# One adaLN block on one core: the shared PSUM steps in a new order, both output projections at the end of the second block, blocks of 9, 10, 9 and 8 steps

## The reference, cut to what matters

```python
mod = (silu(c) @ wmod).reshape(32, 6, 1, 128)       # sa, ca, ga, sb, cb, gb for each batch
ga, gb = sign(.) * max(abs(.), 0.25)
h = layernorm(x) * (1 + ca) + sa
q, k, v = h @ Wq, h @ Wkv                           # 16 heads of 64
s = (q * 64**-0.5) @ k.T;  p = exp(s - rowmax(s)), 0 above the diagonal
x = x + ga * ((p @ v / (sum(p) + 1e-8)) @ Wo + bo)
h = layernorm(x) * (1 + cb) + sb
fp4(t): per 16 channels scale = max|t| / 6; round t / scale to {0, .5, 1, 1.5, 2, 3, 4, 6}; times scale
gate, up = fp4(h) @ fp4(w_gate).T, fp4(h) @ fp4(w_up).T       # 352 hidden channels
x = x + gb * (fp4(silu(gate) * up) @ fp4(w_down).T)
```

## Time and profile before

| what | value |
|---|---|
| median of 3 runs | 1419.69 us (1419.22 to 1420.4) |
| the profiled execution's own time | 1420.77 us |
| its span from first to last instruction | 1418.8 us |
| granted TensorE clock, mean | 0.982 of full speed |
| PE (matmul) busy | 1268.3 us, 89% |
| DVE (VectorE) busy | 1010.3 us, 71% |
| ACT (ScalarE) busy | 836.0 us, 59% |
| POOL (GpSimd) busy | 826.5 us, 58% |
| exponentials, L559 ACT | 1024, mean 432 ns |
| row maxima, L730 DVE | 256, mean 1219 ns |
| normalisation, L429 and L431 POOL | 256 of mean 400 ns and 768 of mean 462 ns |

### The profile page before, as it was taken

One profiled execution on the slowest core, in us unless ns is written; L12 is line 12 of the kernel. 1 busy time (PEld: TensorE's weight loads), 2 busy tenths in 40 slices (PEclk: granted clock), 3 DMA queues, 4 the chain that ended last, 5 costly groups with the idle time before them and its releaser, 6 DMA issues.

```text
span 1418.8 us, 34191 instructions
## 1 busy us (share of the span) xinstructions
PE 1268.3 (89%) x10194; PEld 1045.9 (74%) x10194; DVE 1010.3 (71%) x2565; ACT 836.0 (59%) x2885; POOL 826.5 (58%) x1582
## 2 busy tenths in 40 slices
PE   5989999999999999999999999999999999999963
PEld 3778777777877777877777877777787777787752
DVE  5667777777777777777777777777777777777664
ACT  3666655665655656656666665566566565665630
POOL 2545656655656666655566565665565656665543
PEclk9999999999999999999999999999999999999985
DMA  3000000000000000000000000000000000000000
GB/s 96 16 18 19 8 20 20 17 20 20 4 20 20 17 20 20 7 18 20 20 17 20 19 5 20 20 17 20 20 4 20 20 17 20 20 6 14 18 18 10
DMA packets 38057, 26.54 MB, mean 19 GB/s; under 512 B 2800, under 2 KB 33392, under 8 KB 38032
## 3 DMA queue, kind: packets, MB, share of 16 engines
q1 hardware_dynamic: 38032, 26.23, 6.5%
HBM read 21.94 MB, written 4.28 MB: 18 GB/s over the span
## 4 chain that ended last, share of the span: by engine, by line
POOL 48%; issue 36%; PE 8%; DVE 3%; ACT 2%; POOLq 2%; DMA 1%; SPq 0%; DVEq 0%; ACTq 0%
POOL probs L431 21%; POOL qy L75 6%; POOL qy L73 5%; POOL probs L429 5%; POOL hq L77 3%; PE ps_m L818 2%; POOL rstd L439 2%; POOL h2a L469 2%; POOL xq L77 1%; POOL x_keep L486 1%; POOL x_gb L459 1%; PE ps_s L913 1%; PE ps_o L940 1%; PE ps_m L797 1%; PE ps_m L864 1%
## 5 line engine op out<-in xcount | busy, mean ns | idle before, releaser
L559 ACT ACTIVATE probs<-ps_s,neg_max 128x128 f32<-128x128 f32 (+1 forms) x1024 | 426.0, 432 | 404.9 <-PE ps_s L922 404.9
L431 POOL TENSOR_SCALAR probs<-probs,r_den 128x256 f32<-128x256 f32 (+1 forms) x768 | 341.8, 462 | 0.0
L429 POOL TENSOR_TENSOR probs<-probs,r_den 128x128 f32<-128x128 f32 x256 | 102.5, 400 | 401.8 <-DVE r_den L739 401.8
L730 DVE TENSOR_REDUCE neg_max<-ps_s 128x4 f32<-128x1024 f32 x256 | 304.2, 1219 | 20.2 <-PE ps_s L913 17.2
L656 DVE COPY probs_t<-ps_m 128x512 f32<-128x512 f32 x256 | 176.3, 689 | 134.4 <-PE ps_m L797 134.4
L913 PE MATMUL ps_s<-qk 64*128 64x256 f32 x2048 | 258.3, 391 | 0.4 <-ACT qk L525 0.4
L797 PE MATMUL ps_m<-ident,probs 128*128 128x128 f32 x1536 | 232.4, 274 | 3.9 <-DVE probs_t L656 2.4
L913 PEld LDWEIGHTS ps_s<-qk 64*128 64x128 f32 x2048 | 188.3, 188 | 42.8 <-ACT probs L559 10.9
L559 ACT ACTIVATION_READ_ACCUMULATOR probs<-ps_s,neg_max 128x1 f32 x1024 | 219.2, 214 | 0.0
L940 PE MATMUL ps_o<-probs_t,v 128*64 128x256 f32 (+1 forms) x2048 | 196.0, 333 | 14.3 <-ACT o_t L551 14.3
L940 PEld LDWEIGHTS ps_o<-probs_t,v 128*64 128x64 f32 x2048 | 132.3, 137 | 91.5 <-issue 58.5
(11 more groups left out here) (107 smaller groups left out, 1695.0 us busy)
## 6 DMA issues: line engine op xcount, KB each, us to landing
mod_a<-mod_rows SPq DMA_DIRECT2D x32, 256.0 KB, 3.4
x_in<-L_attn_x SPq DMA_DIRECT2D x32, 128.0 KB, 2.1
x_res<-L_attn_x SPq DMA_DIRECT2D x32, 128.0 KB, 2.1
out<-y_out SPq DMA_DIRECT2D x32, 128.0 KB, 2.9
mod_b<-mod_rows SPq DMA_DIRECT2D x32, 64.0 KB, 3.0
wkv<-L_attn_Wkv SPq DMA_DIRECT2D x2, 512.0 KB, 7.1
wq<-L_attn_Wq SPq DMA_DIRECT2D x1, 512.0 KB, 4.0
wo<-L_attn_Wo SPq DMA_DIRECT2D x1, 512.0 KB, 8.4
```

The costliest lines, as they stand in the source:

```text
L429: nc.gpsimd.tensor_tensor(cols, cols, r_den[:, u % 4, 0:1].to_broadcast([P, P]), ALU.mult)
L431: ins = nc.gpsimd.tensor_scalar(cols, cols, r_den[:, u % 4, s:s + 1], 1.0, ALU.mult, ALU.mult)
L559: ins = nc.scalar.activation(probs[:, u % 4, h, t * P:(1 + 2 * t) * P], ps_s[:, 2 * (u % 2) + h, t * N:t * N + (1 + t) * P], ACT.Exp, bias ...
L730: nc.vector.tensor_reduce(neg_max[:, u % 4, :], ps_s[:, 2 * (u % 2):2 * (u % 2) + 2, :].rearrange("p b (t j) -> p (b t) j", t=2), AX.X, AL ...
```

## The change

The order of the shared steps, of the reads that follow them, and of the other work of ScalarE, VectorE and GpSimd is changed. The instructions, their sizes, the DMA list and the number of shared steps (36) are the same. Both wo steps stand at the end of block 1; blocks have 9, 10, 9 and 8 steps. In blocks 1 to 3 the third t comes before the second qk. On VectorE, the second layer norm's statistics and xn2 move ahead in block 2, both hidden_scales and hidden_magic follow later steps of their blocks, and the quantisation of h2 comes before the reads of down. On GpSimd the rounding of xq moves from block 0 of the next iteration to the end of block 3, rounding of the hidden halves from blocks 2 and 3 to blocks 1 and 3, and h2 from block 3 to block 2. On ScalarE the copy of o_t in block 1 comes later, in block 2 it comes before xt. The three steps that prepare the feed-forward weights (once, in iteration 1) take other places.

```diff
-        PLACES = {
-            (0, 3): ("xqt", 2, 0), (0, 4): ("v", 0, 0), (0, 7): ("gate", 2, 0), (0, 8): ("up", 2, 0),
-            (1, 3): ("wo", 1, 0), (1, 4): ("gate", 2, 1), (1, 7): ("v", 0, 1), (1, 8): ("up", 2, 1),
-            (2, 3): ("wo", 1, 1), (2, 4): ("v", 0, 2), (2, 7): ("v", 0, 3), (2, 8): ("xt", -1, 0),
-            (3, 3): ("hqt", 2, 0), (3, 4): ("hqt", 2, 1), (3, 7): ("down", 2, 0), (3, 8): ("down", 2, 1)}
...
+        SHARED = (
+            ("t0", "qk0", "t1", ("v", 0, 0), ("xqt", 2, 0), "qk1", "t2", ("gate", 2, 0), ("v", 0, 1)),
+            ("t0", "qk0", "t1", ("up", 2, 0), ("gate", 2, 1), "t2", "qk1", ("up", 2, 1), ("wo", 1, 0), ("wo", 1, 1)),
+            ("t0", "qk0", "t1", ("v", 0, 2), ("hqt", 2, 0), "t2", "qk1", ("v", 0, 3), ("xt", -1, 0)),
+            ("t0", "qk0", "t1", ("hqt", 2, 1), "t2", "qk1", ("down", 2, 0), ("down", 2, 1)))
...
+        WEIGHT_PLACES = [(0, 7), (1, 3), (1, 4)]
...
-                    if j == 0 and has.prev2:
...
-                        quantize_round(nc.gpsimd, Steps(pool, xq_round, ROUND_STEPS, i - 2), xq, 2 * P // BLOCK, scale[0],
-                                       qy[0], qm[0])
...
-                    if j in (2, 3) and has.prev2:
-                        round_hidden(i - 2, j - 2)
-                    if j == 3 and has.prev:
+                    if j == 2 and has.prev:
+                        rstd(i - 1, ln2_pool, x1_steps, X1_STEPS * i, mv2, var2, rstd2)
+                    if j in (1, 3) and has.prev2:
+                        round_hidden(i - 2, (j - 1) // 2)
...
+                    if has.attn:
+                        normalize(i, 2 * j)
...
+                    if j == 2 and has.prev:
                         pool.wait_ge(xn2_ready, 2 * i)
...
+                    if j == 3 and has.prev:
+                        pool.wait_ge(xq_steps, QUANT_STEPS * i)
+                        if has.prev2:
+                            pool.wait_ge(xqt_full, i - 1)
+                        quantize_round(nc.gpsimd, Steps(pool, xq_round, ROUND_STEPS, i - 1), xq, 2 * P // BLOCK, scale[0],
+                                       qy[0], qm[0])
...
                         exponentials(2 * j, 1)
-                    if has_out and j == 1:
-                        out_copy()
-                    for n in (0, 1, 2, 3):
+                    first = 5 if j == 2 else 4
+                    for n in range(first):
                         shared_reads(n)
                     if has.attn:
                         exponentials(2 * j + 1, 0)
-                    shared_reads(4)
-                    shared_reads(5)
+                    for n in range(first, 6):
+                        shared_reads(n)
+                    if j == 1 and has.prev:
+                        out_copy()
                     if has.attn:
                         exponentials(2 * j + 1, 1)
-                    for n in (6, 7, 8):
+                    for n in range(6, 8):
                         shared_reads(n)
-                    if has_out and j != 1:
+                    if j != 1 and has.unit(2 * (j - 2)):
                         out_copy()
+                    for n in range(8, len(SHARED[j])):
+                        shared_reads(n)
...
                     shared_reads(j, 0)
+                    if j == 2 and has.prev:
+                        dve.wait_ge(x1_steps, X1_STEPS * (i - 1) + 2)
+                        layer_norm_stats(x1, stats2, mv2, x1_steps, X1_STEPS * (i - 1) + 2)
                     shared_reads(j, 2)
+                    shared_reads(j, 3)
                     if has.attn:
                         denominators(2 * j)
...
+                    shared_reads(j, 4)
+                    if j == 1 and has.prev2:
+                        hidden_scales(i - 2, 0)
                     if j == 0 and has.next:
...
+                    if j == 1 and has.prev2:
+                        hidden_magic(i - 2, 0)
+                    if j == 2 and has.prev2:
+                        hidden_scales(i - 2, 1)
+                    if j == 2 and has.prev:
+                        dve.wait_ge(ln2_pool, 2 * i)
+                        normalized([xn2[:, t * P:t * P + P] for t in range(2)], x1, mv2, rstd2, xn2_ready)
+                    if j == 2 and has.prev2:
+                        hidden_magic(i - 2, 1)
                     if j == 1 and has.next:
...
                     if j == 3 and has.prev:
                         dve.wait_ge(h2_ready, i)
...
+                    for n in range(5, len(SHARED[j])):
+                        shared_reads(j, n)
```

More of the change, by code:

```diff
@@ L301, in iterations, with place_of @@
                 body(i)
-        PLACES = {
[3 rows of a table removed]
-            (3, 3): ("hqt", 2, 0), (3, 4): ("hqt", 2, 1), (3, 7): ("down", 2, 0), (3, 8): ("down", 2, 1)}
[L309 to L316, removed]
+        SHARED = (
[4 rows of a table added]
+        def place_of(j, step):
+            part = int(step[-1]) if isinstance(step, str) else 0
+            if not isinstance(step, str):
+                return step
+            if step[0] == "t":
+                return ("t", 0, 3 * (j - 1) + part) if j > 0 else ("t", 1, 3 * (PAIRS - 1) + part)
+            return ("qk", 0, 2 * (j + 1) + part) if j < PAIRS - 1 else ("qk", -1, part)
+        PLACES = {(j, n): place_of(j, step) for j in range(PAIRS) for n, step in enumerate(SHARED[j])}
+        assert len(PLACES) % 3 == 0
+        WEIGHT_PLACES = [(0, 7), (1, 3), (1, 4)]
         def shared_steps(i):
@@ L487, in body @@
                     if j == 2 and has.prev:
-                        rstd(i - 1, ln2_pool, x1_steps, X1_STEPS * i, mv2, var2, rstd2)
+                        pool.wait_ge(xn2_ready, 2 * i)
+                        xn2_v, h2a_v, h2_v = (t[:, :].rearrange("p (t c) -> p t c", t=2) for t in (xn2, h2a, h2))
+                        nc.gpsimd.tensor_tensor(h2a_v, xn2_v, both_tiles(mod_a[:, 2, :]), ALU.mult).then_inc(h2a_ready, 1)
+                        pool.wait_ge(h2a_ready, i)
+                        if has.prev2:
+                            pool.wait_ge(xq_steps, QUANT_STEPS * (i - 1))
+                        nc.gpsimd.tensor_tensor(h2_v, h2a_v, both_tiles(mod_a[:, 3, :]), ALU.add).then_inc(h2_ready, 1)
+                    if j == 3 and has.prev:
+                        pool.wait_ge(xq_steps, QUANT_STEPS * i)
+                        if has.prev2:
+                            pool.wait_ge(xqt_full, i - 1)
+                        quantize_round(nc.gpsimd, Steps(pool, xq_round, ROUND_STEPS, i - 1), xq, 2 * P // BLOCK, scale[0],
+                                       qy[0], qm[0])
             def round_hidden(b, k):
@@ L546, in out_copy @@
                     def out_copy():
-                        if j == 2 and has.prev:
-                            act.wait_ge(wo_full, 2 * i)
                         at = 2 * ((j - 2) % PAIRS)
@@ L563, in exponentials @@
                         ins.then_inc(exp_done, 1)
-                    has_out = has.unit(2 * (j - 2))
                     if has.attn:
@@ L767, in body @@
                         normalized([xn[:, t, :] for t in range(2)], x_in, mv1, rstd1, xn_ready)
[L768 to L776, removed]
                     if j == 3 and has.prev:
@@ L958, in body @@
                         mask(2 * j + 1, 1)
-                    for n in range(2, 9):
+                    for n in range(2, len(SHARED[j])):
                         at_place(j, n)
```

10 lines of the change are left out of this document (removed).

## The result

| | before | after |
|---|---|---|
| median | 1420.05 us | 1362.88 us |
| ratio, 95% interval | | 0.9599 (0.958 to 0.9618) |
| profiled span | 1418.8 us | 1359.9 us |
| granted clock, mean | 0.982 | 0.988 |

What follows compares the result with a forecast made beforehand. TensorE's idle time was taken as the bound. Period 38.0 + 0.2 + 0.15 + 1.6 = 40.0 us against 42.15, 2.1 less over 30 periods (63 us), plus 4 in the drain: 1354 us, range 1318 to 1387.

Steps and rivals of the forecast that it cites:

- What bounds: TensorE over the four blocks: its idle time is the gain to be had, in a period of 42.15 us.
- All four waits: TensorE's waits per period: mask 1.61 us, xq transposes 0.59, output projection 0.45, values 0.44.
- Quantise before down: Block 3: earlier quantisation starts block 0's maximum at 1.6 to 1.9 us, removing the mask's 1.61, 1.7 with weight load.
- xq round: GpSimd's rounding of xq at the end of block 3 removes the 0.59 us wait, 0.75 with its weight load.
- Hidden round 1: GpSimd in block 3: hqt comes at 6.8 us in place of 5.44, a stall of 1.35 us.
- the meeting: Block 2: VectorE's xn2 and magic overlap GpSimd's h2a and h2, 0.5 to 0.7 us each time, together 1.0 to 1.4.
- The sum: Period 40.0 us against 42.15, 2.1 less over 30 periods, 63 us, plus 4 in the drain: 67 us.
- the chain: VectorE and GpSimd delays up to hqt in block 3, with 0.25 us elsewhere: 1.6 a period, bounds 0.5 to 2.7.
- the rest of the period: The period apart from the 1.6 us chain: 38.0 without waits, plus 0.2 in block 0 and 0.15 in block 1.
- The last block and the drain: End of the run, 59 us at granted clock 0.62: 4 us gained, 0 to 8, as quantisation leaves the downs' back.
- Rival A: VectorE and GpSimd interleave, no meeting over 0.1 us: chain 0.5, period 38.9, 1321 us; chance 0.20.
- Rival C: GpSimd's round 0 holds t0 of block 2, slack 0.4 us: stall 3.1, period 43.1, 1447 us, slower; chance 0.07.

Runs made afterwards that it cites:

- e2: Changed kernel with VectorE's quantisation of h2 put back behind both reads of down; 1417.54 us, ratio 0.998.
- e9: Changed kernel's step order, but xn2 and h2 in block 3, quantisation behind the downs, round of xq in block 0; 1381.28 us, ratio 0.9721.
- e3: Changed kernel with GpSimd's round of xq put back to block 0 of the next iteration; 1365.42 us, ratio 0.9607.
- e1: Changed kernel with GpSimd's two h2 instructions cut from 128 to 8 columns of each token half, the rest constant; 1337.39 us, ratio 0.9411.
- e6: Changed kernel with GpSimd's round of hidden half 1 ahead of the normalisation of unit 5 in block 3; 1366.27 us, ratio 0.9626.
- e4: Changed kernel with VectorE's hidden_magic for half 0 moved behind both projections' reads at the end of block 1; 1483.81 us, ratio 1.0441.
- e8: As e7, with GpSimd's round of hidden half 1 also moved to the end of its block 2; 1357.49 us, ratio 0.9563.
- e10: Changed kernel with VectorE's xn2 ahead of hidden_scales in block 2 and GpSimd's h2 ahead of the normalisation of unit 4; 1357.94 us, ratio 0.9555.
- e5: Changed kernel with the second hqt step two places later in block 3; 1359.65 us, ratio 0.9577.
- e7: Changed kernel with VectorE's hidden_magic for half 1 ahead of xn2, and GpSimd's h2 in block 3 behind the half-1 round; 1372.55 us, ratio 0.9673.

## Why the prediction was right, and where it was off

*What bounds.* Right: PE busy is unchanged and the gain is its idle time. All four waits of the earlier trace rows are gone, also that of the values, of which 0.2 was forecast to stay.

*Quantise before down.* Right, first maximum at 1.50 (forecast 1.6 to 1.9); e2 shows that with the rest of the change nothing is left without it, and e9 that without the early h2 39 us remain even so.

*xq round.* Failed as a term. The prediction gave its move 0.75 us; e3 shows 0 in the steady part. The wait went because quantisation ends earlier, and either place of the round would do. In the sum this made no error, since it counted the waits that vanish, but it named the wrong cause for one.

*Hidden round 1 and the meeting.* Right in mechanism, and hqt's time is right: 6.87 us into block 3 (forecast 6.8), its wait 1.2 (forecast 1 to 1.4), block 3 at 10.1 (10.0). e1 takes the meeting away and the loss with it. The terms inside were less exact, and that they cancel is luck: L65 and L66 lost 0.84 us together where 1.0 to 1.4 was priced, magic 1 ended 1.52 us into block 3 (forecast 1.75), but from there to POOL's start on the normalisation 0.59 us passed in place of 0.35. The price of each meeting, half way between nothing and full, was near because POOL's instruction had already begun: L65 had 0.55 us of h2a before it and lost 0.41. L62's mean did not rise (0.53 before, 0.52 after), which was forecast too. The Trainium skill (SBUF — State Buffer, section on the two separate sides) has the rule, an exclusive lock for the whole instruction; the traces agree (four columns held for 0.91 us in e6). The row of 0.41 at 720.66 in the earlier trace rows was not DVE alone, as the prediction and the title of those rows have it: POOL's normalisation of the earlier trace rows ran from 720.26 to 721.77 beside it. There it was POOL that lasted longer, 1.51 us for its three steps in place of the usual 1.28, which looks like a meeting with the other loser; no run isolates it.

*The sum.* Off in two terms, with opposite signs. The steady gain was 1.6 us a period, not 2.1: block 1 takes 12.14 (forecast 11.9) since two projections, 32 matmuls, take 3.74 us to the next scores, where I had taken 3.4, twice the 1.70 from one projection's start to the next step in the trace before; blocks 0 and 3 are 0.2 and 0.1 longer. That makes 48 us from iteration 2 on in place of 63. Put in the prediction's terms, the chain, priced at 1.6, was not too cheap: hqt came 1.43 us later than wanted. The term that was too small is the rest of the period, 38.0 and 0.35 of small waits, which measured 39.1. The last block and the drain took 60.5 us, before 69.2: 8.7 and not 4, outside the 0 to 8 of the prediction too. Before:

```profile
1349.61:1418.80 69.19, 35.62 (x207) 27.81 (x206) 34.52 (x90) 12.23 (x36) 29.17 (x44) 0.67 0.05 14
```

Part of it is waits: quantisation is in front of down, and the projections and xqt come earlier. Another part is the clock. PE's busy time there fell from 35.62 to 32.11 us for nearly the same matmuls, at a granted clock of 0.76 in place of 0.67; before, the clock stood at half from 1367 to 1373, and the values at 1369.59 took 2.83 us, after they took 1.52 at 1316.39. So up to 3.5 of the 8.7 us are the clock's, a term that the prediction lacks. No run parts the two. Iterations up to 1 gave 1.8. Together 59 in the profiled spans (1418.8 less 1359.9).

*Rival A.* e1 came to 1337 us, a period of 39.6, and not to A's 1321 and 38.9, although hqt waited only 0.4 us in it. A's chain of 0.5 was right for that case; the rest of the period was too small in A as it was in the sum.

*Rival C.* Its mechanism is real (e4), but its price was not. The round came 4.0 us later and t0 2.26, so t0 had 1.8 us of slack, and not the 0.4 of the prediction. The normalisation of unit 2 ends 2.7 us into block 2 and t0 is wanted at 3.6, but each transpose waits only for its own one of the four instructions (line 826 of the kernel before), so t0 can start before the last is done. What made e4 slower than C's 1447 us, with less waiting than C had, is the clock, and the rest of the period, which was too small in C as well.

What stays open: e8 and e10 each save 5 us by different moves; whether they add was not tried. Nor does a run show why the clock fell in e4 and stood at 1.00 in the other runs' steady blocks, where one wait was as long as 1.6 us (e9).

## What to carry to other kernels

Before a move, write down for each engine the latest start that its consumer allows (here 2.09 us for the maximum, 5.44 for hqt, 3.6 for t0) and compare that slack with what the move adds; e5 and e6 failed where one engine's list was left out of that account, and e7 because a shorter block 3 also brings forward the moment at which block 0 wants its maximum. When VectorE and GpSimd are both given SBUF work at the same moment, count each overlap as a wait of up to the rest of the other's instruction, however small one's own is, and place the overlap where the held engine has slack. When a new wait comes close behind another, look at the granted clock of the steps after it before pricing the waits alone. Credit a gain to a wait only after asking whether another part of the change removes it already.

## What the runs showed of the hardware

A VectorE instruction on 128x4 elements, 0.16 us alone, lasted 0.91 us beside a GpSimd instruction of 0.93 (e6). Held time is counted as busy: VectorE's busy share rose from 71% to 81% with the same instructions. Row maxima and copies, which read PSUM, kept their means (1219 and 689 ns before, 1218 and 689 after). TensorE's granted clock fell to 0.50 for about 3 us in each period of e4, behind idle stretches of 0.92 and 1.10 us with 0.4 us of work between them; in the before kernel single idle stretches of 1.61 us left it at 1.00.
